# A quarter of a depthwise convolution moved from TensorE and VectorE to ScalarE and GpSimd

## The reference

```python
x = x + L0(_gn(x), ...)              # _gn: mean and variance over groups of channels and all pixels
xz = einsum('bhwc,ec->bhwe', x, in_proj_w)
xc, z = split(xz, 2, axis=-1)        # 192 channels each
xc = conv_general_dilated(xc, conv_w, (1, 1), 'SAME', feature_group_count=192)   # 3 x 3, one filter a channel
xa = silu(xc + conv_b)               # and silu(z) for the gate
```

## Time and profile before

| | us |
|---|---|
| median of 3 runs (11366.33 to 11380.14) | 11378.12 |
| the profiled execution, its time | 11368.93 |
| its span, first to last instruction | 11366.8 |
| the front, to ScalarE's last SiLU | 601.15 |

### The profile page before, as it was taken

The page is one execution under the profiler, slowest core; times in us unless marked ns, Lnnn a source line. Parts: engine busy times, 40 slices in busy tenths (PEclk is TensorE's granted clock), DMA queues, the critical chain, the costliest instruction groups (busy, mean ns, idle before and its releaser), DMA issues. The chain is left out here.

```text
span 11366.8 us, 332308 instructions
## 1 busy us (share of the span) xinstructions
PE 9731.8 (86%) x136268; PEld 6088.9 (54%) x136268; DVE 10107.4 (89%) x6303; ACT 8498.9 (75%) x15618; POOL 9153.2 (81%) x3978
## 2 busy tenths in 40 slices
PE   8978888888878888888888888888888887999999
PEld 5644444444444444444444444444444444787788
DVE  7879999999999999999999999999999996555554
ACT  3478888888888888888888888888888884444443
POOL 1169999999999999999999999999999996333330
PEclk9989999999999999999999999999999998999999
DMA  3366676677666766776677667766776664212210
GB/s 101 110 167 169 174 184 175 171 176 182 171 172 175 184 171 172 177 182 169 173 177 186 167 173 178 180 169 172 183 180 167 175 177 108 54 46 68 64 50 12
DMA packets 562160, 1716.31 MB, mean 151 GB/s; under 512 B 147651, under 2 KB 148451, under 8 KB 558857
## 3 DMA queue, kind: packets, MB, share of 16 engines
q1 hardware_dynamic: 499464, 1483.21, 52.5%
q10 hardware_dynamic: 61184, 211.85, 6.0%
HBM read 1319.08 MB, written 375.39 MB: 149 GB/s over the span
## 5 line engine op out<-in xcount | busy, mean ns | idle before, releaser
L989 POOL TENSOR_TENSOR HC<-H,crep 128x1024 f32<-128x1024 f32 x3072 | 7193.9, 2382 | 370.9 <-PE psum L718 370.6
L782 DVE TENSOR_TENSOR_SCAN H<-E,car,psum 128x1024 f32<-128x1024 f32 x2112 | 4875.1, 2337 | 96.0 <-POOL HC L989 37.7
L696 PE MATMUL psum<-diag,dluT 128*32 128x128 f32 x98304 | 3294.1, 288 | 797.5 <-DVE H L782 755.6
L866 ACT ACTIVATE E<-dlr,am 128x1024 f32<-128x1024 f32 x2816 | 3202.6, 1144 | 910.6 <-DVE H L782 898.9
L696 PEld LDWEIGHTS psum<-diag,dluT 128*32 128x32 f32 x98304 | 2821.1, 116 | 1886.0 <-DVE H L782 1601.9
L850 ACT ACTIVATE diag<-idn,blt 128x128 f32<-128x128 f32 x8192 | 2514.9, 391 | 52.0 <-PE psum L696 49.5
L718 PE MATMUL psum<-HC,sely 128*32 128x512 f32 x12288 | 2188.1, 621 | 155.9 <-POOL HC L989 149.9
L782 DVE TENSOR_TENSOR_SCAN H<-E,psum 128x1024 f32<-128x1024 f32 x704 | 1583.7, 2277 | 58.1 <-POOL HC L989 34.3
L760 DVE TENSOR_TENSOR psum<-dur,psum 128x1024 f32<-128x1024 f32 x1280 | 1545.2, 1207 | 19.4 <-DMA dur<-scr_dlu 19.4
L664 PE MATMUL psum<-sx,selb 96*128 96x512 f32 x2560 | 956.6, 455 | 373.6 <-DVE H L782 371.4
L664 PEld LDWEIGHTS psum<-sx,selb 96*128 96x128 f32 x2560 | 387.0, 191 | 1134.8 <-DVE H L782 671.8
(11 more groups left out here) (143 smaller groups left out, 9970.5 us busy)
## 6 DMA issues: line engine op xcount, KB each, us to landing
dur<-scr_dlu SPq DMA_DIRECT2D x3072, 128.0 KB, 3.8
dlr<-scr_dl SPq DMA_DIRECT2D x3072, 128.0 KB, 3.7
crep<-scr_bc SPq DMA_DIRECT2D x1024, 256.0 KB, 5.2
scr_dlu<-dlu SPq DMA_DIRECT2D x256, 384.0 KB, 3.3
scr_yk<-yt ACTq DMA_DIRECT2D x256, 384.0 KB, 3.5
brep<-scr_bc SPq DMA_DIRECT2D x512, 128.0 KB, 2.9
scr_dl<-dlt ACTq DMA_DIRECT2D x128, 384.0 KB, 3.0
scr_dl<-yt ACTq DMA_DIRECT2D x128, 384.0 KB, 4.6
```

Source lines behind the costliest of these rows:

```text
L696: r = e.matmul(bank("unit", un)[32 * q:32 * q + 32, i * 128:(i + 1) * 128], dluT[:, m % 2, i, 32 * j:32 * j + 32], diag[:, i, at + q, :], ...
L782: e.tensor_tensor_scan(H[:, un % NH, ::step], decay[:, ::step], drive[:, ::step], init, ALU.mult, ALU.add).then_inc(scan_done)
L866: e.activation(o, dlr[:, slot(m, j), :], ACT.Exp, scale=am[:, ae:ae + 1]).then_inc(exp_done)
L989: e.tensor_tensor(HC[:, un % NHC, :], H[:, un % NH, :], crep[:, GREP.index(g), :], ALU.mult).then_inc(hc_done)
```

## The change

In each batch, q = 0 of the first half and q = 3 of the second half are made in another way; the second not in the last batch. ScalarE multiplies the padded projection by a tap's weight (`terms`, one `mul` a tap on 96 x 1024 elements; the first tap goes into `acc`, the others into a ring of 4 buffers `term`), and GpSimd adds the 8 further terms to `acc` one after the other (`add`). ScalarE applies SiLU to `acc` (`sum_silu`) and SyncE stores it. Since the first half needs its own projection for this, TensorE makes 3 narrow jobs more (8, 8 and 1 rows) behind the wide ones, and ScalarE copies them to a small padded image `xn`. TensorE's two convolution jobs of q = 0 are gone, VectorE's `wide(b, 3)` too but for the last batch. TensorE's product for the next batch's statistics stands, as before, behind the gates of q = 0, and VectorE's `stats(b + 1)`, as before, behind `wide(b, 0)`.

GpSimd's queue in a batch is now 8 additions, the split of the next batch, 8 additions. ScalarE's terms are laid in at written places. The core of the diff:

```diff
@@ tensor
             for r in range(8):
                 project(b, NJOB * b + r, C, r * 8)
+            for r in range(NNARROW):
+                project(b, NJOB * b + NWIDE + r, 0, r * 8, 8 if r < 2 else 1)
             for q in range(4):
-                for r in range(2):
-                    conv(b, conv_job(b, q, r), q * 16 + r * 8)
+                if q:
+                    for r in range(2):
+                        conv(b, conv_job(b, q, r), q * 16 + r * 8)
@@ vector
-            for q in range(4):
+            for q in range(4 if b == NB - 1 else 3):
                 wide(b, q)
                 if q == 0 and b + 1 < NB:
                     stats(b + 1)
@@ scalar
+        def terms(b, which, first, last):
+            un = summed(b, which)
+            x, w, row = (xc[b % 2], cww, 48) if which else (xn[b % 2], cwn, 0)
+            e.wait_ge(job_out, NJOB * b + (NWIDE if which else NWIDE + NNARROW))
+            for t in range(first, last):
+                if t == 0:
+                    if b:
+                        e.wait_ge(acc_stored[which], 16 * b)
+                    o = acc[:, which, :]
+                else:
+                    i = 8 * un + t - 1
+                    if i >= NTMP:
+                        e.wait_ge(term_added, i - NTMP + 1)
+                    o = term[:, i % NTMP, :]
+                e.mul(o.rearrange("p (h w) -> p h w", w=HW), x[:, row + t // 3:row + t // 3 + 16, t % 3:t % 3 + HW],
+                      w[:, t:t + 1]).then_inc(term_made)
+
+        def sum_silu(b, which):
+            e.wait_ge(term_added, 8 * summed(b, which) + 8)
+            x = acc[:, which, :]
+            e.activation(x, x, ACT.Silu, bias=cb[:, which:which + 1]).then_inc(acc_out)
...
+            if b:
+                terms(b - 1, 1, 5, 9)
+            terms(b, 0, 0, 3)
             for q in range(4):
-                i = conv_slot(b, q)
...
+                if q:
+                    if q == 1:
+                        terms(b, 0, 3, 7)
+                        if b:
+                            sum_silu(b - 1, 1)
+                    elif q == 2:
+                        terms(b, 0, 7, 9)
+                    elif b + 1 < NB:
+                        terms(b, 1, 0, 3)
+                    i = slot_at["conv", b, q]
+                    slot_free(e, i)
...
                 if q == 1 and b + 1 < NB:
                     normalise(b + 1)
+                if q == 2:
+                    sum_silu(b, 0)
+            if b + 1 < NB:
+                terms(b, 1, 3, 5)
@@ pool
+        def add(b, which):
+            un = summed(b, which)
+            x = acc[:, which, :]
+            for t in range(1, 9):
+                i = 8 * un + t - 1
+                e.wait_ge(term_made, 9 * un + t + 1)
+                if t > 1:
+                    e.wait_ge(term_added, i)
+                e.tensor_tensor(x, x, term[:, i % NTMP, :], ALU.add).then_inc(term_added)
+
+        split(0)
+        for b in range(NB):
+            add(b, 0)
+            if b + 1 < NB:
+                split(b + 1)
+                add(b, 1)
```

More of the change, by code:

```diff
@@ L61, in pre_phase @@
     sem = namer(nc, ctx, "pre")
-    win, cwr, cww, cb, gmat, eps = (T(n, s) for n, s in (
-        ("win", [C, 2 * ND]), ("cwr", [C, 9, C]), ("cww", [C, 9]), ("cb", [C, 2]), ("gmat", [C, C]), ("eps", [C, 1])))
+    win, cwr, cww, cwn, cb, gmat, eps = (T(n, s) for n, s in (
+        ("win", [C, 2 * ND]), ("cwr", [C, 9, C]), ("cww", [C, 9]), ("cwn", [C, 9]), ("cb", [C, 2]), ("gmat", [C, C]),
+        ("eps", [C, 1])))
     wtap = [T(f"wtap{i}", [C, 9, C], F32R) for i in range(2)]
@@ L68, in pre_phase @@
     xc = [T(f"xc{i}", [C, PADW, PADW]) for i in range(2)]
+    xn = [T(f"xn{i}", [C, 18, PADW]) for i in range(2)]
+    NTMP = 4
+    term = T("term", [C, NTMP, 1024])
+    acc = T("acc", [C, 2, 1024])
     NX = 6
@@ L95, in pre_phase, with wide_unit, summed @@
     stored = [sem(f"stored{i}") for i in range(NX)]
[L97 to L104, removed]
+    term_made = sem("term_made")
+    term_added = sem("term_added")
+    acc_out = sem("acc_out")
+    acc_stored = [sem(f"acc_stored{i}") for i in range(2)]
+    ring = []
+    for b in range(NB):
+        for q in range(4):
+            if q:
+                ring += [("conv", b, q)]
+            if q < 3 or b == NB - 1:
+                ring += [("wide", b, q)]
+            ring += [("gate0", b, q), ("gate1", b, q)]
+    slot_at = {job: i for i, job in enumerate(ring)}
     def conv_job(b, q, r):
-        return NJOB * b + 8 + 6 * q + r
+        return NJOB * b + NWIDE + NNARROW + 4 + 6 * (q - 1) + r
     def gate_job(b, half, q, r):
-        return NJOB * b + 8 + 6 * q + 2 + 2 * half + r
+        return NJOB * b + NWIDE + NNARROW + (6 * q if q else 0) + 2 * half + r
+    def wide_unit(b, q):
+        return 3 * b + q
+    def summed(b, which):
+        return 2 * b + which
     def slot_free(e, i):
@@ L116, in sync @@
     def sync(e):
-        for t, n in ((win, "winT"), (cwr, "cwr"), (cb, "cb"), (cww, "cww"), (gmat, "gmat")):
+        for t, n in ((win, "winT"), (cwr, "cwr"), (cb, "cb"), (cww, "cww"), (cwn, "cwn"), (gmat, "gmat")):
             e.dma_start(t[:], S[n]).then_inc(weights_in, 16)
@@ L128, in store_wide, with store_sum @@
         def store_wide(b, q):
-            e.wait_ge(wide_out, 4 * b + q + 1)
-            store(wide_slot(b, q), "xa", b, 1, q)
+            e.wait_ge(wide_out, wide_unit(b, q) + 1)
+            store(slot_at["wide", b, q], "xa", b, 1, q)
+        def store_sum(b, which):
+            e.wait_ge(acc_out, summed(b, which) + 1)
+            q = 3 if which else 0
+            e.dma_start(S["xa"][b, which, :, q * 1024:(q + 1) * 1024], acc[:, which, :]).then_inc(acc_stored[which], 16)
         load(0)
@@ L135, in sync @@
             for q in range(4):
[L136 to L139, removed]
+                if q:
+                    e.wait_ge(job_out, conv_job(b, q, 1) + 1)
+                    store(slot_at["conv", b, q], "xa", b, 0, q)
+                    store_wide(b, q - 1)
                 for half in range(2):
                     e.wait_ge(job_out, gate_job(b, half, q, 1) + 1)
-                    store(gate_slot(b, half, q), "sz", b, half, q)
+                    store(slot_at[f"gate{half}", b, q], "sz", b, half, q)
+                if q == 1 and b:
+                    store_sum(b - 1, 1)
                 if q == 1 and b + 2 < NB:
                     load(b + 2)
+                if q == 3:
+                    store_sum(b, 0)
         store_wide(NB - 1, 3)
         for x in range(NX):
-            e.wait_ge(stored[x], 16 * len(range(x, 16 * NB, NX)))
+            e.wait_ge(stored[x], 16 * len(range(x, len(ring), NX)))
+        e.wait_ge(acc_stored[0], 16 * NB)
+        e.wait_ge(acc_stored[1], 16 * (NB - 1))
     def tensor(e):
@@ L157, in bank, with project @@
             return ps[job % NBANK][0:C, :]
-        def project(b, job, col, h0):
-            o = bank(job)
+        def project(b, job, col, h0, rows=8):
+            o = bank(job)[:, 0:rows * HW]
             split_product(e, o, [w[:, col:col + C] for w in wins],
-                          [x[:, h0 + 1:h0 + 9, 1:HW + 1] for x in xp[b % 2]]).then_inc(job_done)
+                          [x[:, h0 + 1:h0 + 1 + rows, 1:HW + 1] for x in xp[b % 2]]).then_inc(job_done)
         def conv(b, job, h0):
@@ L169, in conv @@
             i.then_inc(job_done)
[L171 removed]
+        e.wait_ge(weights_in, 96)
         group(0)
@@ L205, in wide @@
         def wide(b, q):
-            i = wide_slot(b, q)
-            acc = xs[:, i % NX, :].rearrange("p (h w) -> p h w", w=HW)
-            n = 9 * (4 * b + q)
+            i = slot_at["wide", b, q]
+            o = xs[:, i % NX, :].rearrange("p (h w) -> p h w", w=HW)
+            n = 9 * wide_unit(b, q)
             slot_free(e, i)
@@ L256, in scalar @@
         normalise(0)
-        e.wait_ge(weights_in, 80)
-        e.wait_ge(pads_set, 24)
+        e.wait_ge(weights_in, 96)
+        e.wait_ge(pads_set, 30)
         for b in range(NB):
-            for r in range(8):
+            for r in range(NWIDE + NNARROW):
                 job = NJOB * b + r
                 e.wait_ge(job_done, job + 1)
[L263 to L266, removed]
-            for q in range(4):
-                i = conv_slot(b, q)
[L269 to L276, removed]
+                if r < NWIDE:
+                    if b >= 2:
+                        e.wait_ge(tap_done, 27 * (b - 1))
+                        e.wait_ge(term_made, 18 * (b - 1))
+                    o, rows = xc[b % 2][:, r * 8 + 1:r * 8 + 9, 1:HW + 1], 8
+                else:
+                    n = r - NWIDE
+                    rows = 8 if n < 2 else 1
+                    o = xn[b % 2][:, n * 8 + 1:n * 8 + 1 + rows, 1:HW + 1]
+                e.copy(o, ps[job % NBANK][0:C, 0:rows * HW].rearrange("p (h w) -> p h w", w=HW)).then_inc(job_out)
+            if b:
+                terms(b - 1, 1, 5, 9)
+            terms(b, 0, 0, 3)
+            for q in range(4):
```

(16 more changed lines are left out.)

19 lines of the change are left out of this document (11 added, 8 removed).

## The result

The median after is 11489.53 us (4 runs, 11481.33 to 11500.09) against 11374.48 before (4 runs): a ratio of 1.0102, 95% interval 1.0085 to 1.012, so 115 us slower. The profiled execution took 11481.33 us, 112 more than the one before.

A forecast was written before the change was run, and what follows sets the result against it. VectorE and GpSimd, by turns, were to bound the front at 89.9 us a batch; its end moves from 601.15 to 736.5, so 11368.9 + 135 = 11504, and the median, 9.2 above, is 11514 us; range 11440 to 11610.

The forecast's parts named there:

- VectorE and GpSimd take turns: In the front, taps and GpSimd's instructions exclude each other; together their work is 83 us a batch, over today's 69.7.
- TensorE idles at the grouping: TensorE reaches the next batch's statistics product before VectorE is ready and idles at the least 9 us a batch.
- the walk: One batch followed from grouping product to grouping product, engine by engine: a batch lasts 89.9 us, 20 more than today.
- The clock: TensorE runs slow for a while after an idle stretch: 2.7 us charged for each stretch.
- The sum: Batch 0, six periods and batch 7 put the front's last SiLU at 736.5 instead of 601.15: 135 us more.
- No exclusion: Rival: additions and taps don't exclude each other, only the statistics' cover is lost: 73 us a batch, 11391 us; chance 0.07.
- Faster: Rival: TensorE keeps the front's pace, 90 us less, 11288 us; chance 0.04.
- Dearer additions: Rival: GpSimd's additions take 3.13 us each, by L1679, instead of 2.35: 11604 us; chance 0.10.
- VectorE wins the turns: Rival: VectorE goes first and GpSimd starves: a period of 75 us, 11405 us; chance 0.06.
- The signs: Expected in the profile: TensorE idle some 20 us a batch, 8-tap groups of 20 us, taps near 2.9, additions 2.4 to 3.5.
- ScalarE: In the front ScalarE gets 18 products, about 55 us a batch against 33, hidden but for what stands in the order.

The follow-up runs named there:

- experiment 2: The kernel after, with VectorE's statistics instructions, aggregation and release of the grouping ahead of the first quarter's taps instead of behind them: 11460 us, ratio 1.0081 to the kernel before.
- experiment 3: The kernel after, with GpSimd's additions cut to one column and the statistics ahead of the first quarter's taps: 11272 us, ratio 0.9916 to the kernel before.
- experiments 5 and 6: The kernel after with taps' sum in accumulator banks and statistics ahead of the first quarter's taps: 11303 us; 6 also moves only the first half's quarter: 11291 us.

## Why the prediction was right

The forecast was 11514 us, the measured time is 11490; in the front 135 us more were forecast and 118.6 came. By its steps:

- *VectorE and GpSimd take turns.* Right, and it is what sets the batch. Additions take 3192 ns in the middle, 2351 at the least; a tap after release 1.1 us (the last of the group at 125.09 ends at 147.39, the last addition beside it at 146.30). An addition and a tap in turns take 3.28 us (19.68 / 6), where I had 3.45: part of the one lies beside the other. The first product of a quarter, which reads one operand, waits too, 2959 ns at the most for 749 in the middle. The rows of one line each:

```profile
L245 DVE TENSOR_SCALAR xs<-xc,cww x25: 742/749/2959, 44.0 to 707.3; 96x1024 f32<-96x1024 f32 x25
...
L392 POOL TENSOR_TENSOR acc<-acc,term x120: 2351/3192/3467, 52.3 to 688.0; 96x1024 f32<-96x1024 f32 x120
```

- *TensorE idles at the grouping.* It does, for up to 26.8 us a batch, and, as in the walk, it lies beside the path that sets the batch: experiment 2 took it away and gained 3.2 us a batch. Only with the turns gone does it set the pace; it then costs 14.0 us a batch (71.5 to 57.5). TensorE's own work was put at 58.2 us; its sum, 69.7 - 11.6 + 0.3, gives 58.4, and 57.5 was measured in experiment 3.
- *The clock.* 2.7 us an idle stretch was charged; the first 54 matmuls behind the grouping take 15.27 us in the batch shown, where the next 54 take 13.03; 2.2 more, and beside the path.
- *The walk.* 89.9 us a batch were forecast, 87.5 measured. In the batch shown: grouping to the second quarter's start 2.9 (forecast 4.1), the quarters 19.4 and 28.6 (19.8 and 29.0), ScalarE's tail to the copies 5.05 (5.8), copies to taps 1.7 (1.9), first quarter 25.3 (23.6), statistics with the grouping 5.5 (5.8). The term that was mis-sized most is the first quarter, 1.7 us too short: the walk had five additions in turn with its taps and six fall there (19.68 us in the batch shown), and its first product takes 2.95 us where the walk has 2.45 with the wait. The other six terms err the other way, some 3.3 us together; the largest is the first, 1.2 us, since ScalarE loads its table at 136.32, during its wait, and not behind it. So the walk is closer than its terms are, by errors of both signs. This batch lasts 88.35; the next lasts 86.2, since its third quarter's taps take 25.73 us, not 27.87.
- *The sum.* 2.4 us x 6 batches = 14.4 of the 16.7 us by which the front was over-estimated; the rest of the program was taken as unchanged and was 6 us shorter, less than the 16 us by which it varies over the runs here. Together that is most of the 24 us between forecast and median. The last SiLU ends at 719.76, not 736.5:

```profile
718.61 1.15 ACT L283 ACTIVATE xs<-xs,cb 96x1024 f32<-96x1024 f32 x1 [5.94 <-DVE xs L248]
```

- *Rivals.* "No exclusion" was priced at 73 us a batch and 11391; with the exclusion taken away by the banks it is 74.0 and 11384, with small additions 71.5 and 11365. "Faster" was priced at 11288 if TensorE kept the pace; with both obstacles gone it is 11272. Dearer additions (3.13 alone) is refuted: alone they take 2.35. "VectorE wins the turns" is refuted by the additions' times beside the taps.
- *The signs.* TensorE waits 26 us for L228 in the batch shown, where some 20 and more were named, and the additions' mean of 3.05 us lies in the 2.4 to 3.5 named. The taps' mean is 2.66 us, not 2.9, and of the three groups of taps in the batch one is under the 20 us named (18.62).
- *ScalarE.* Its 18 products at 1.15 us are hidden but for its tail of 5.05 us, as said; it is busy for 33.93 of 60 us in the second window above, against 28.25 in the earlier trace rows. Only when all else is gone (experiments 5 and 6) does its own work hold TensorE.

## What to carry to other kernels

Two engines that each have room are not free together: look in the trace for one instruction that lasts as long as another engine's, and sum the work of both as if it were one engine's. When work is taken off the engine that sets the pace, list what stood behind it in its queue and what that work covered; here the statistics. And take obstacles away together as well as one by one: 16 and 3 us apart were 30 together.

## What the runs showed of the hardware

- An operand in an accumulator bank frees VectorE from GpSimd: taps 1285 ns and additions 2385 at the same time, against 2658 and 3049 with both operands in the common memory (means, waits included). The first product with its output there costs 1283 ns in place of 747.
- VectorE's one-operand product of 747 ns also waits for GpSimd's addition (up to 2959 ns in the kernel after), while the statistics instructions (L223, 4.83 us for 8 beside additions) don't. The Trainium skill's page "SBUF — State Buffer", section "SBUF: two separate sides", names instructions in a two-port mode beside those with two inputs there; the waits agree, but no run here shows in which mode the product runs. The same page of the Trainium skill, section "A bandwidth-pool intuition that's wrong (but worth ruling out)", gives some 115 ns between VectorE's end and the going on of a blocked GpSimd, which there has a transfer's descriptors to write. In these turns no such gap is to be seen: an addition and a tap take 3.28 us, less than 2.35 + 1.28 = 3.63.
- A one-column addition takes 186 ns on GpSimd at the least; the mean of 591 and the most, 1177, come of waiting for VectorE's tap. So GpSimd's instruction waits for VectorE's as VectorE's does for GpSimd's, however short the one that waits.
